# Text rows normalised by ScalarE, VectorE's token-stage order following TensorE's products, and another bank order in attention's first product

## The chip, the cores and the metric

The kernel runs on one core of a Trainium2 chip. The metric is the device time of one execution in microseconds (us). The core has five engines, each with its own queue of instructions that it takes strictly in order: TensorE (PE in the profile; its weight loads are PEld), VectorE (DVE), ScalarE (ACT), GpSimd (POOL) and SyncE (SP), which here only issues transfers. They are ordered against each other by semaphores alone: an instruction raises one when it ends, and another engine's queue stands at a wait until it is high enough.

## The reference

One transformer layer over 16 sequences of 69 tokens of width 256, in fp32. A sequence is one class token, 36 image patches and 32 text rows.

```
h = tokens(x)                      # per patch: 768 values
    x = layernorm(x; ln1_g, ln1_b) @ W + bias
    x = layernorm(x; ln2_g, ln2_b) + pe
h = concat(cls, h, txt)            # 16 x 69 x 256
h = h + attention(layernorm(h))    # one head, rotated q and k, softmax
h = h + ffn(layernorm(h))          # shared expert + best 2 of 8 experts
```

The layernorm in front of attention has no gain and no shift: `(h - mean) / sqrt(var + eps)`. For the text rows it depends on the input alone, so it can be done while the patches are still being worked on.

## The kernel before

The whole layer is one program. Its stages are tokens (0 to some 44 us), attention (to some 85 us), the shared expert with the router (to some 160 us), and the routed experts, 25 tiles of 128 rows (to the end). Every stage is a list of calls per engine, written out by hand; the order of the calls in each engine's list is the order of its queue. Between engines there are only the semaphores.

**Token stage.** The 576 patch rows lie in five tiles i = 0 to 4, the first of 64 rows and four of 128. For each tile:

- VectorE: `tok_stats(i)`, mean and variance of 768 values (L1175); GpSimd: `tok_root(i)`, the power -1/2 (L501, by L474); VectorE: `tok_shift(i)`, -mean times root (L1184); ScalarE: `tok_norm(i)`, scale and bias in place (L650).
- TensorE: `tok_transposes(i)`, six transposes (L859, by L853) into banks 2 and 3 for even i, 6 and 7 for odd i; ScalarE: `tok_turned(i)` takes them out with gain and shift of the first layernorm (L656); it counts `t_aff`.
- TensorE: `tok_product(i)`, bias and six products (L876, L881) into bank 4 for even i and 5 for odd i; it counts `t_mm`.
- VectorE: `tok_stats2(i)` (L1190): statistics of the product, then L1199, which takes it out of the bank with the second gain and counts `t_gain`. GpSimd: `tok_root2(i)`. VectorE: `tok_end(i)` (L1209), times the root, plus `pe`, into which GpSimd's `place_rows_of(i)` (L492) has added the second shift; it counts `t_done`.
- VectorE: `attention_front(i)` (L1214), statistics of the finished token rows; GpSimd: `attention_root(i)`; VectorE: `attention_bias(i)` (L1224); ScalarE: `attention_norm(i)` (L670).
- TensorE: `attention_transposes(k)` (L884): k = 0 to 3 are the four tiles of text rows, k = 4 to 8 the five token tiles, into bank 0 or 1. ScalarE: `attention_copy(k)` (L676) writes the high part (rounded to fp32r), VectorE: `attention_low(k)` (L1240) the rest, and counts `a_low`. Transposes k wait for `a_low` k - 1, since they write the bank of k - 2.

**Text rows.** `xtxt` holds 512 text rows as four tiles of 128 x 256. VectorE does `text_stats` (L1227) behind `tok_shift(2)`. GpSimd's `text_norm` (L481) takes one root for all four, waits for it, and normalises the tiles one after another (L486); each counts `x_normed`. It stands between `tok_root(2)` and `tok_root(3)`.

**Attention's weights.** wq, wk and wv are split in the same way, GpSimd making the high part (L496, L498), VectorE the low part (L1246, L1247, in one call `attention_weights`, counting `a_w` once).

**Attention's first product.** The 16 sequences are four groups of four (276 columns). `attention_qk(g)` (L898) has two halves `eo`, each of two products (q and k) of six matmuls; half 1 writes banks 4 and 5, half 0 banks 2 and 3, and half 1 comes first. Group 0 waits ahead of everything for `a_low` 6, `a_w` 1, `t_aff` 5 and `t_gain` 5. VectorE's rotation, `attention_turn(0)` (L1257, L1258) and `attention_rope(0)` (L1261, L1262), waits for all four products; `attention_v(0)` and `attention_scores(0)` follow on TensorE.

**Order around the change.** GpSimd's list begins at L526. After `attention_root(4)` it waits for `a_w`, `t_mm` 5 and `t_done` 5, and then splits the first experts' weights in pieces of 128 x 512 (L442, L443) between the roots of attention's second layernorm (`flat_root(g)`). `load_weights(n)` (L432) issues the transfer of 1 MB of expert weights into one of two stages. ScalarE's list begins at L725, TensorE's at L1037, VectorE's at L1314. SP issues all input transfers in a fixed order and then, tile by tile behind `t_done`, the copies of the token rows into `h` (`place_images`, L351).

## Time and profile before

| | |
|---|---|
| median of 3 runs | 341.75 us (339.48 to 342.25) |
| the profiled execution: its own time | 340.2 us |
| its span in the profile | 338.4 us |
| TensorE busy | 301.1 us (89%) |
| VectorE, ScalarE, GpSimd busy | 159.8, 145.3, 210.0 us |

The profiled execution is one more run beside the three. Its span goes from the first instruction to the last, and all times within the profile count from the span's start; around the span lie 1.8 us of the execution's own time. In a timeline, consecutive instructions of one line are merged into a row with their count; the start is that of the first, the time is from there to the end of the last. "Idle before" is how long the engine had stood, and the arrow names what ended that. The duration of a matmul record overlaps with the next one's. PEclk is TensorE's granted clock as a share of 2.4 GHz.

### The profile page before, as it was taken

The numbers are of one execution on the slowest core, as the hardware profiler recorded it, in microseconds if no ns is written. First come the engines' busy times: TensorE is split into PE (matmuls) and PEld (weight loads), VectorE is DVE, ScalarE is ACT, GpSimd is POOL, SyncE is SP. The second block draws the span as 40 slices with busy tenths as digits, with TensorE's granted clock in tenths as the row PEclk, the third lists the DMA queues.
The fourth block names the chain that finished last, engine by engine and source line by source line (L and its number), as shares of the span: only waits on it lengthen the run. The fifth ranks groups of instructions, "written<-read, shape, count | busy, mean of one in ns | idle before, by whom it ended". The sixth has DMA issues, their size and how long they took to land.

```text
span 338.4 us, 6655 instructions
## 1 busy us (share of the span) xinstructions
PE 301.1 (89%) x2049; PEld 269.5 (80%) x2050; DVE 159.8 (47%) x402; ACT 145.3 (43%) x327; POOL 210.0 (62%) x168
## 2 busy tenths in 40 slices
PE   0879788998897969999899999999999999999970
PEld 0456587887795969998699989998999899899960
DVE  3558867888853399473223332433233233323220
ACT  2647313375978533642444344333433343344210
POOL 2476373148882000755988988898888899335551
PEclk9997979999999999999999999999999999999997
DMA  7955404002464230375453364255333633224522
GB/s 235 314 104 158 144 26 158 0 27 63 153 211 157 97 119 2 108 239 193 164 169 108 137 201 163 52 172 186 114 111 101 175 57 47 34 44 47 64 33 31
DMA packets 21926, 39.91 MB, mean 118 GB/s; under 512 B 2914, under 2 KB 18227, under 8 KB 19603
## 3 DMA queue, kind: packets, MB, share of 16 engines
q0 software_dynamic: 7456, 25.43, 28.0%
q1 hardware_dynamic: 14162, 14.03, 13.4%
q10 hardware_dynamic: 288, 0.20, 0.2%
q8 instruction: 11, 0.18, 0.2%
q14 instruction: 9, 0.07, 0.1%
HBM read 28.84 MB, written 6.93 MB: 106 GB/s over the span
## 4 chain that ended last, share of the span: by engine, by line
PE 41%; POOL 12%; DMA 12%; issue 8%; DVE 7%; ACT 2%; POOLq 2%; SPq 0%; DVEq 0%; ACTq 0%
DMA out_tokens<-xy_all,dest 11%; PE ps L978 9%; PE ps L979 9%; PE ps L980 9%; PE ps L1028 7%; POOL ring L443 6%; PE ps L853 4%; POOL ring L442 3%; POOL out_tokens L590 2%; PE ps L948 2%; POOLq L587 1%; PE ps L1100 1%; DVE h L1286 1%; DVE ps L1258 1%; DVE qk L1257 1%
## 5 line engine op out<-in xcount | busy, mean ns | idle before, releaser
L443 POOL TENSOR_TENSOR ring<-stage,ring 128x512 fp32r<-128x512 f32 (+2 forms) x30 | 76.2, 2541 | 2.5
L1549 DVE TENSOR_TENSOR hgT<-ps,hgT 128x512 fp32r<-128x512 f32 x50 | 32.2, 687 | 72.2 <-ACT hgT L843 72.2
L978 PE MATMUL ps<-ring,hgT 128*128 x200 | 58.0, 290 | 2.1 <-DVE xy_all L1555 1.5
L590 POOL DMA_INDIRECT out_tokens<-xy_all,dest x25 | 39.5, 1582 | 27.5 <-DMA out_tokens<-xy_all,dest 15.6
L980 PE MATMUL ps<-ring,hgT 128*128 x200 | 55.9, 279 | 0.0
L979 PE MATMUL ps<-ring,hgT 128*128 x200 | 55.9, 279 | 0.0
L835 ACT ACTIVATE hg<-ps 128x512 f32<-128x512 f32 x50 | 29.9, 599 | 47.6 <-PE ps L980 47.6
L580 POOL DMA_INDIRECT xy_all<-normalized_tokens,dest x25 | 24.9, 997 | 38.8 <-DVE dest L1511 31.4
L978 PE MATMUL ps<-ring,xgT 128*128 x100 | 41.3, 413 | 1.1 <-issue 0.6
L442 POOL TENSOR_SCALAR ring<-stage 128x512 fp32r<-128x512 f32 (+2 forms) x30 | 38.5, 1284 | 2.6 <-PEq L1114 2.4
L978 PEld LDWEIGHTS ps<-ring,hgT 128*128 128x128 f32 x200 | 37.6, 188 | 2.6 <-issue 2.6
L979 PE MATMUL ps<-ring,xgT 128*128 x100 | 39.4, 394 | 0.0
L980 PE MATMUL ps<-ring,xgT 128*128 x100 | 39.2, 392 | 0.0
L979 PEld LDWEIGHTS ps<-ring,hgT 128*128 128x128 f32 x200 | 37.7, 188 | 0.0
L980 PEld LDWEIGHTS ps<-ring,hgT 128*128 128x128 f32 x200 | 37.6, 188 | 0.0
L818 ACT ACTIVATE xgT<-ps 128x256 fp32r<-128x256 f32 x25 | 9.6, 386 | 53.7 <-PE ps L853 53.7
L1555 DVE TENSOR_SCALAR xy_all<-ps,gate 128x256 f32 (+1 forms) x25 | 12.1, 484 | 38.6 <-PE ps L980 38.6
L1028 PE MATMUL ps<-ring,hid 128*128 128x256 f32 x216 | 29.5, 282 | 0.2 <-DVE base L1378 0.2
L1028 PEld LDWEIGHTS ps<-ring,hid 128*128 128x128 f32 x216 | 28.3, 189 | 0.6 <-issue 0.5
L843 ACT ACTIVATE hgT<-ps 128x512 fp32r<-128x512 f32 x50 | 27.1, 599 | 2.6 <-PE ps L853 2.6
L853 PE MATMUL ps<-mats,hg 128*128 128x128 f32 x200 | 25.9, 272 | 0.0
L853 PEld LDWEIGHTS ps<-mats,hg 128*128 128x128 f32 x200 | 23.3, 140 | 3.2
(193 smaller groups left out, 591.0 us busy)
## 6 DMA issues: line engine op xcount, KB each, us to landing
stage<-in_w_up POOLq DMA_DIRECT2D x9, 1024.0 KB, 5.5
stage<-in_w_dn POOLq DMA_DIRECT2D x9, 1024.0 KB, 5.6
xg<-xy_all SPq DMA_DIRECT2D x25, 128.0 KB, 2.7
xp<-in_patches SPq DMA_DIRECT2D x4, 384.0 KB, 7.6
normalized_tokens<-hn SPq DMA_DIRECT2D x4, 276.0 KB
residual_tokens<-h SPq DMA_DIRECT2D x4, 276.0 KB
ring<-in_tok_w SPq DMA_DIRECT2D x1, 768.0 KB, 7.0
base<-residual_tokens SPq DMA_DIRECT2D x2, 384.0 KB, 4.1
```

Source lines behind the costliest of these rows:

```text
L442: link(nc.gpsimd.tensor_scalar(hi, stage[:, part, c0:c1], 1.0, 0.0, ALU.mult, ALU.add))
L443: return nc.gpsimd.tensor_tensor(lo, stage[:, part, c0:c1], hi.bitcast(F32), ALU.subtract)
L580: pool.indirect_dma_start(xy_all[:, t, :], None, xn_d, bass.IndirectOffsetOnAxis(ap=dest[:, t:t + 1].bitcast(U32), axis=0)).then_inc(rows_ ...
L590: pool.indirect_dma_start(out, bass.IndirectOffsetOnAxis(ap=dest[:, t:t + 1].bitcast(U32), axis=0), xy_all[:, t, :], None, compute_op=ALU. ...
L835: nc.scalar.activation(hg[:, 1 - c, 512 * half:512 * (half + 1)], ps[:, hidden_bank + half, :], ACT.Gelu).then_inc(e_act, 1)
L843: nc.scalar.activation(hgT[:, c, 0, 4 * half:4 * half + 4, :], ps[:, turned_bank + half, :].rearrange("p (k t) -> p k t", k=4), ACT.Copy). ...
L853: return nc.tensor.transpose(o, i, ident[0:n, 0:n])
L978: nc.tensor.matmul(o, a[0], b[0], start=n == 0, stop=False)
L979: nc.tensor.matmul(o, a[0], b[1], start=False, stop=False)
L980: last = nc.tensor.matmul(o, a[1], b[0], start=False, stop=n == len(pairs) - 1)
L1028: last = nc.tensor.matmul(ps[:, down_bank[j], 0:D], a[x], b[y], start=f == 0 and m == 0, stop=f == KF - 1 and m == 2)
L1549: v.tensor_tensor(hgT[:, c, 1, 4 * half:4 * half + 4, :], ps[:, turned_bank + half, :].rearrange("p (k t) -> p k t", k=4), hgT[:, c, 0, 4 ...
```

## The change

It does three things. Of the text rows GpSimd keeps the root alone; VectorE works out -mean times root for all four tiles in one operation (`text_shift`, into the new `xnb`), and ScalarE normalises two tiles behind `tok_norm(2)` and two behind `attention_copy(1)`. The low part of attention's weights is made in three calls (half of the q and k weights by `w` each, then v), each counting `a_w`, and VectorE's and GpSimd's lists are put in another order; on GpSimd `load_weights(0)`, `load_weights(1)`, `attention_weights` and `place_rows_of(i)` move. ScalarE takes `attention_copy(2)` ahead of `tok_turned(3)`. In `attention_qk(0)` the half on banks 2 and 3 comes first, the wait for `t_gain` stands ahead of the second half, and the wait for the v weights stands ahead of `attention_v(0)`. TensorE's list is the same.

```diff
--- before.py
+++ after.py
@@ -160,6 +160,7 @@
         xst = sb("xst", [P, NG, 6], where=slots12)
         xmv = sb("xmv", [P, NG, 2], where=slots12)
         xrs = sb("xrs", [P, NG], where=slots12)
+        xnb = sb("xnb", [P, NG], where=slots12)
         pr = sb("pr", [SEQ, GB, SEQ], where=slots12)
         asm = sb("asm", [SEQ, 3, GB], where=slots12)
         prT = sb("prT", [SEQ, GB, SEQ], where=slots12)
@@ -213,7 +214,7 @@
         first_in = sem("first_in")
         pe_in, rope_in, text_in = [sem(f"pe_in{i}") for i in range(NPT)], sem("rope_in"), sem("text_in")
         rows_of_text_in = sem("rows_of_text_in")
-        x_stats, x_rstd, x_normed = sem("text_stats"), sem("text_rstd"), sem("text_normed")
+        x_stats, x_rstd, x_shift, x_normed = (sem(n) for n in ("text_stats", "text_rstd", "text_shift", "text_normed"))
         img_in = [sem(f"img_in{i}") for i in range(NPT)]
         a_stats, a_rstd, a_normed, a_tr, a_hT = (sem(n) for n in ("a_stats", "a_rstd", "a_normed", "a_tr", "a_hT"))
         a_norm_in, a_low, a_whi, a_w = sem("a_norm_in"), sem("a_low"), sem("a_whi"), sem("a_w")
@@ -478,13 +479,9 @@
                 r = AROWS[i]
                 root(ars[0:r, i:i + 1], amv[0:r, i, 1:2], r, a_rstd)
 
-            def text_norm():
+            def text_root():
                 pool.wait_ge(x_stats, 1)
                 root(xrs[:, :], xmv[:, :, 1], P, x_rstd)
-                pool.wait_ge(x_rstd, 1)
-                for j in range(NG):
-                    nc.gpsimd.tensor_scalar(xtxt[:, j, :], xtxt[:, j, :], xmv[:, j, 0:1], xrs[:, j:j + 1], ALU.subtract,
-                                            ALU.mult).then_inc(x_normed, 1)
 
             def place_rows_of(i):
                 pool.wait_ge(pe_in[i], 16 * (1 if i == 0 else 2))
@@ -527,29 +524,29 @@
             tok_root(0)
             tok_root(1)
             tok_root(2)
-            text_norm()
+            text_root()
             tok_root(3)
             pool.wait_ge(tok_vec_in, 32)
             place_rows_of(0)
             tok_root2(0)
+            load_weights(0)
             tok_root(4)
-            load_weights(0)
+            place_rows_of(1)
             attention_root(0)
-            place_rows_of(1)
+            attention_weights()
             tok_root2(1)
+            place_rows_of(2)
+            load_weights(1)
             attention_root(1)
-            attention_weights()
-            place_rows_of(2)
+            place_rows_of(3)
             tok_root2(2)
-            load_weights(1)
+            place_rows_of(4)
             attention_root(2)
-            place_rows_of(3)
             tok_root2(3)
             attention_root(3)
-            place_rows_of(4)
             tok_root2(4)
             attention_root(4)
-            pool.wait_ge(a_w, 1)
+            pool.wait_ge(a_w, 3)
             pool.wait_ge(t_mm, NPT)
             pool.wait_ge(t_done, NPT)
             piece(0, 0)
@@ -670,6 +667,12 @@
                 nc.scalar.activation(tn[0:r, i, :], tt[0:r, i, :], ACT.Identity, bias=anb[0:r, i:i + 1],
                                      scale=ars[0:r, i:i + 1]).then_inc(a_normed, 1)
 
+            def text_norm(j0, j1):
+                act.wait_ge(x_shift, 1)
+                for j in range(j0, j1):
+                    nc.scalar.activation(xtxt[:, j, :], xtxt[:, j, :], ACT.Identity, bias=xnb[:, j:j + 1],
+                                         scale=xrs[:, j:j + 1]).then_inc(x_normed, 1)
+
             def attention_copy(k):
                 act.wait_ge(a_tr, k + 1)
                 for o, i in placings(k, 0):
@@ -728,14 +731,16 @@
             tok_turned(0)
             tok_turned(1)
             tok_norm(2)
+            text_norm(0, 2)
             tok_norm(3)
             tok_turned(2)
             attention_copy(0)
             attention_copy(1)
+            text_norm(2, 4)
             tok_norm(4)
             attention_norm(0)
+            attention_copy(2)
             tok_turned(3)
-            attention_copy(2)
             attention_copy(3)
             attention_copy(4)
             attention_norm(1)
@@ -898,12 +903,13 @@
             def attention_qk(g):
                 te.wait_ge(a_low, NG + LAST_TILE[g] + 1)
                 if g == 0:
-                    te.wait_ge(a_w, 1)
+                    te.wait_ge(a_w, 2)
                     te.wait_ge(t_aff, NPT)
-                    te.wait_ge(t_gain, NPT)
                 else:
                     te.wait_ge(a_rope, g)
-                for eo in (1, 0):
+                for eo in (1, 0) if g else (0, 1):
+                    if g == 0 and eo == 1:
+                        te.wait_ge(t_gain, NPT)
                     if g >= 3 and eo == 0:
                         te.wait_ge(f_lo, g - 2)
                     for w in range(2):
@@ -914,6 +920,8 @@
 
             def attention_v(g):
 
+                if g == 0:
+                    te.wait_ge(a_w, 3)
                 if g >= 1:
                     te.wait_ge(a_exp, g)
                     te.wait_ge(a_pTs, g)
@@ -1234,18 +1242,24 @@
                 link(last)
                 v.tensor_scalar(xmv[:, :, 1], xmv[:, :, 1], EPS, None, ALU.add).then_inc(x_stats, 1)
 
+            def text_shift():
+                dve.wait_ge(x_rstd, 1)
+                v.scalar_tensor_tensor(out=xnb[:, :], in0=xmv[:, :, 0], scalar=-1.0, in1=xrs[:, :], op0=ALU.mult,
+                                       op1=ALU.mult).then_inc(x_shift, 1)
+
             def attention_low(k):
                 dve.wait_ge(a_hT, k + 1)
                 for (o, i), (high, _) in zip(placings(k, 1), placings(k, 0)):
                     last = v.tensor_tensor(o, i, high.bitcast(F32), ALU.subtract)
                 last.then_inc(a_low, 1)
 
-            def attention_weights():
-
+            def attention_weights(n):
                 dve.wait_ge(a_whi, 1)
-                v.tensor_tensor(wqk2[:, 1, :, :, :], wqk[:, :, :, :], wqk2[:, 0, :, :, :].bitcast(F32), ALU.subtract)
-                v.tensor_tensor(wv2[:, 1, :, :], wvs[:, :, :], wv2[:, 0, :, :].bitcast(F32),
-                                ALU.subtract).then_inc(a_w, 1)
+                if n < 2:
+                    v.tensor_tensor(wqk2[:, 1, n, :, :], wqk[:, n, :, :], wqk2[:, 0, n, :, :].bitcast(F32),
+                                    ALU.subtract).then_inc(a_w, 1)
+                else:
+                    v.tensor_tensor(wv2[:, 1, :, :], wvs[:, :, :], wv2[:, 0, :, :].bitcast(F32), ALU.subtract).then_inc(a_w, 1)
 
             def attention_turn(g):
                 if g == 0:
@@ -1319,6 +1333,7 @@
             tok_shift(2)
             text_stats()
             tok_stats(3)
+            text_shift()
             tok_shift(3)
             tok_stats2(0)
             tok_stats(4)
@@ -1329,26 +1344,28 @@
             attention_low(1)
             attention_bias(0)
             tok_stats2(1)
+            attention_weights(0)
             tok_end(1)
             attention_front(1)
+            attention_weights(1)
+            attention_bias(1)
             attention_low(2)
+            tok_stats2(2)
             attention_low(3)
-            attention_bias(1)
-            tok_stats2(2)
-            attention_weights()
-            attention_low(4)
             tok_end(2)
             attention_front(2)
+            attention_low(4)
             attention_bias(2)
+            attention_weights(2)
             tok_stats2(3)
             attention_low(5)
             tok_end(3)
             attention_front(3)
+            tok_stats2(4)
             attention_bias(3)
-            tok_stats2(4)
-            attention_low(6)
             tok_end(4)
             attention_front(4)
+            attention_low(6)
             attention_bias(4)
             attention_turn(0)
             attention_rope(0)
```

## Rows read from the trace of the kernel before

**Rows 1.** Windows: us, busy of each engine, PEclk, DMA share, GB/s
```profile
45.00:46.00 1.00, 1.00 (x6) 1.00 (x6) 0.52 (x1) 0.00 (x0) 1.00 (x2) 0.50 0.08 21
200.00:320.00 120.00, 120.00 (x829) 109.90 (x829) 39.13 (x71) 45.73 (x89) 93.50 (x52) 1.00 0.42 98
...
```

**Rows 2.** Timeline, TensorE: start, us, what, count, [idle before, releaser]
```profile
12.87 4.91 PE L881 MATMUL ps<-ring,xT 128*64 128x256 f32 x12
...
25.91 0.74 PE L853 MATMUL ps<-mats,xtxt 128*128 128x128 f32 x4 [2.43 <-DVE hT_n L1240]
...
27.21 4.54 PE L881 MATMUL ps<-ring,xT 128*128 128x256 f32 x12
31.59 0.29 PE L853 MATMUL ps<-mats,tn 65*128 65x65 f32 x2
...
33.09 2.86 PE L881 MATMUL ps<-ring,xT 128*128 128x256 f32 x12
...
39.41 0.38 PE L853 MATMUL ps<-mats,tn 128*128 128x128 f32 x2
43.25 0.36 PE L978 MATMUL ps<-hT_n,wqk 128*128 128x276 f32 x1 [3.46 <-DVE tt L1199]
...
53.32 0.38 PE L978 MATMUL ps<-hT_n,wqk 128*128 128x276 f32 x1
...
56.45 0.41 PE L853 MATMUL ps<-mats,pr 69*69 69x69 f32 x4
...
```

**Rows 3.** Timeline, GpSimd, 0 to 72 us
```profile
14.29 1.01 POOL L474 TENSOR_TENSOR xrs<-xmv,half_neg 128x4 f32<-128x4 f32 x1 [2.21 <-DVE xmv L1235]
15.41 4.85 POOL L486 TENSOR_SCALAR xtxt<-xtxt,xmv,xrs 128x256 f32<-128x256 f32 x4
20.23 0.55 POOL L474 TENSOR_TENSOR trs<-tmv,half_neg 128x1 f32<-128x1 f32 x1
20.76 0.71 POOL L492 TENSOR_TENSOR ring<-ring,vecs 64x256 f32<-64x256 f32 x1
...
30.11 1.04 POOL L496 TENSOR_SCALAR wqk<-ring 128x1024 fp32r<-128x1024 f32 x1
...
45.43 0.62 POOL L442 TENSOR_SCALAR ring<-stage 128x512 fp32r<-128x512 f32 x1
...
66.45 1.04 POOL L474 TENSOR_TENSOR rs<-mv,half_neg 69x4 f32<-69x4 f32 x1 [12.27 <-DVE mv L1299]
...
```

**Rows 4.** Timeline, VectorE, 0 to 66 us
```profile
20.81 0.68 DVE L1187 SCALAR_TENSOR_TENSOR tnb<-tmv,trs 128x1 f32<-128x1 f32 x1 [4.64 <-POOL trs L474]
...
22.54 1.00 DVE L1179 BATCH_NORM_STATS2 tst<-xp 128x6 f32<-128x384 f32 x2
...
24.00 0.51 DVE L1209 SCALAR_TENSOR_TENSOR tt<-tt,trs,ring 65x256 f32<-65x256 f32 x1
...
25.21 0.15 DVE L1219 TENSOR_SCALAR amv<-amv 65x1 f32<-65x1 f32 x1
...
32.93 1.22 DVE L1246 TENSOR_TENSOR wqk<-ring,wqk 128x1024 fp32r<-128x1024 f32 x1
...
37.69 0.42 DVE L1196 BATCH_NORM_STATS2 tst<-ps 128x6 f32<-128x256 f32 x1
...
38.82 0.55 DVE L1240 TENSOR_TENSOR hT_n<-ps,hT_n 128x16 fp32r<-128x16 f32 x3
...
48.18 1.31 DVE L1257 TENSOR_TENSOR qk<-ps,rope 128x1104 f32<-128x1104 f32 x1 [2.13 <-PE ps L980]
...
```

**Rows 5.** Timeline, ScalarE, 0 to 66 us
```profile
21.53 1.03 ACT L653 ACTIVATE xp<-xp,tnb,trs 128x768 f32<-128x768 f32 x1 [6.45 <-DVE tnb L1187]
...
42.00 0.60 ACT L670 ACTIVATE tn<-tt,anb,ars 128x256 f32<-128x256 f32 x1 [1.66 <-DVE anb L1224]
...
```

**Rows 6.** Timeline of SP; DMA issues: count, KB, us to landing
```profile
9.37 0.55 SPq L345 DMA_DIRECT2D ring<-in_wv  x1
...
ring<-in_wv SPq DMA_DIRECT2D x1, 256.0 KB, 9.7
...
```

## The prediction

> **What bounds the kernel now.** I read the windows first, then the timelines of the first 66 us engine by engine. From 200 to 320 us TensorE is busy 120.00 of 120.00 us at clock 1.00 [rows 1]: the experts run at TensorE's pace, so nothing in this change shortens them, and they start when the work ahead hands over. The change lies in the first 48 us, where TensorE is not full. Its timeline shows two holes [rows 2]: 2.43 us before the text transposes at 25.91, released by VectorE's low part of the turned rows, and 3.46 us before attention's first product at 43.25, released by VectorE's L1199, the gain of the last token tile. Behind each hole the work runs slowly: the 12 matmul records of the third token product take 4.54 us where the fourth's take 2.86 [rows 2], and in 45 to 46 us the granted clock is 0.50 [rows 1], that is 1.2 GHz where 2.4 was granted before the hole. So in this stretch VectorE sets the time, and the text rows sit at its head: GpSimd takes 4.85 us for four text rows from 15.41, only then the root of tile 3 at 20.23 [rows 3], and VectorE waits 4.64 us for it (from 16.17 to 20.81) [rows 4] and ScalarE 6.45 us (from 15.08 to 21.53) [rows 5].
>
> **The text rows.** GpSimd loses 4.85 us. ScalarE gains four operations of 128x256 with scale and bias; the same form in attention_norm takes 0.60 [rows 5], starts 0.5 apart when they queue, so 2.2 us in two pairs. This form on xtxt isn't in the trace; the bounds are 0 (wholly inside ScalarE's 6.45 us idle) and 4.85 (GpSimd's pace); I take 0, since its first pair needs xrs (14.29 + 1.01 = 15.3) [rows 3] and xnb. xnb is one new VectorE operation of four columns behind tok_stats(3), at 16.2, some 0.15. The new operation can cost 0.15 (shift(3) is held for another reason at that time) or, held by GpSimd like the row discussed next, 0.7; neither moves tok_norm(3) by more than 0.5. ScalarE then: text pair 16.35 to 17.4, tok_norm(3) 17.6 to 18.6, tok_turned(2) and two copies to 21.4, second text pair to 22.4, tok_norm(4) to 23.4. Nothing behind them is late: TensorE needs tile 3 at 22.5, behind its second product, as now.
>
> **VectorE's new order, forward from 16.2.** Root(3) runs 16.25 to 16.8 (0.55 [rows 3]), not from 20.23. Tok_shift(3) is held to 17.5, and here a row counts that is easily missed: tnb at 20.81 took 0.68 us for one column, while GpSimd's L492 ran from 20.76 for 0.71; both ended together [rows 3, 4]. A VectorE operation with two inputs in SBUF stands until GpSimd's running operation has ended. I charge this hold wherever it falls; its bounds are 0 and 1.04, GpSimd's longest operation here [rows 3].
> The Trainium skill, page "SBUF — State Buffer", section "Who interferes with whom", says that the two engines share one pair of ports and that whichever starts first holds it for its whole instruction, so that GpSimd can be the one that waits. The row above agrees for GpSimd first; no row here shows VectorE first. By the rule place_rows_of(2) would be pushed behind attention_weights(0), and my sum would change by 0.3 us at most.
> Steps (start on VectorE; lengths by rows 4): tok_stats2(0) at 17.8, when the first product ends (12.87 + 4.91 [rows 2]), 1.13 (37.69 to 38.82); tok_stats(4) 1.46 (22.54 to 24.00), to 20.4; tok_end(0) and attention_front(0) 1.36 (24.00 to 25.36), to 21.8; shift(4), low(0), low(1) 0.9, to 22.7. Attention_root(0) ends 22.4, but GpSimd then copies wqk for 1.04 [rows 3]: bias(0) ends 23.45. Tok_stats2(1) to 24.6. Attention_weights(0) is half of the 1.22 row [rows 4]: to 25.2. Tok_end(1) is held by place_rows_of(2) (24.9 to 25.6), and with front(1) ends 27.0; weights(1) to 27.6; bias(1) behind root(1) and place_rows_of(3) 28.3; low(2) to 28.7 (ScalarE's copy(2), now ahead of tok_turned(3), is done at 24.4; behind it, as before, it would be 26.5, still in time). There TensorE's attention_transposes(4) can start, now at 31.59 [rows 2]: **2.9 us earlier**.
> Is TensorE ready? Its second text pair comes at 23.2, not 25.91; the third product, 5.68 us from 25.91 to 31.59 with 1.68 lost to the clock (4.54 less 2.86), is through at 27.2. It waits 1.5 us for low(2).
> From transposes(4) on TensorE's queue is full: 31.59 to 39.41 is 7.8 us [rows 2], so transposes(6) come at 36.5. Their inputs are ready (low(3) 30.2 for 32.9; low(4) 32.4 for 36.5).
>
> **Attention's first product.** Today it waits for t_gain of tile 4. Banks 2 and 3 don't hold that product, so with them first only low(5) (35.1), a_w 2 (27.6) and the last turned tile (32) are needed: it starts at 36.85 instead of 43.25. The gap of 3.84 us behind transposes(6) (39.41 to 43.25) shrinks to 0.35: **3.5 us**. The other two banks come 1.56 us later, 38.4; t_gain is there at 36.5 + 1.13 = 37.65. The product itself takes 3.13 at full clock, as qk(1) does (53.32 to 56.45) [rows 2], and ends at 40.0. Against now (43.25 to the rotation at 48.18 [rows 4], 4.9) that is 1.8 less; but bias(4) stands ahead of the rotation in VectorE's queue: tok_end(4) waits for its root (38.0), front(4) ends 39.4, root(4) 39.95, and the weights' first piece, 0.62 [rows 3], holds bias(4) to 40.6. So **1.2 us**. The rotation starts at 40.6 instead of 48.18: 2.9 + 3.5 + 1.2 = **7.6 us**.
>
> **What else moves.** Splitting the weights' low part into three adds two fixed parts of 0.1 us, inside the above. A_w 3 falls at 33.4, ahead of its waiters: the values at 40.4 and GpSimd's pieces at 39.95. GpSimd's first weight load goes from behind root(4) to behind tok_root2(0), about 19.3. The last wide input, wv, is issued at 9.37 and lands 9.7 later, 19.1 [rows 6]; its reader is at 23.4. SP's queue keeps its order and its waits (t_done) fall earlier. Behind 48 us nothing is edited. GpSimd waits 12.27 us for VectorE at 66.45 [rows 3], so its pieces have room, and with experts at TensorE's pace the whole 7.6 should arrive at the end. I charge nothing for it; the bounds are 0 and 7.6 lost.
> The profiled execution took 340.2 us (span 338.4); less 7.6 it gives 332.6. The median shown is 341.75, 1.55 more; less 7.6 it gives 334.15. I forecast between them, **333.4 us**.
>
> **The rivals.** A: a low clock remains. TensorE's hole of 1.5 us is shorter than the two behind which it fell (2.43, 3.46), but they are of one order, and the level was low after both. One fall costs what it cost now, 1.7 us; two 3.4: 335 to 337. Chance 0.16.
> B: the holds don't fall as charged (bias(0) 0.75, tok_end(1) 0.4, bias(1) 0.7, bias(4) 0.6). Then TensorE's third product binds, at 27.2: 1.5 for it and 0.6 for the last: 331.3. Chance 0.14.
> C: the earlier start isn't handed on: a wait on a DMA or on GpSimd's splitting takes its place between 50 and 160 us. Against it: the 12.27 us of room, and no loads bound there. Up to all of 7.6 goes: 337 to 341. Chance 0.07.
> D, the slower side, by the clock alone: the hole before transposes(4) grows past 2.43 us, and the clock stays low to the end of the first value product. Products 3 and 4 cost 1.7 more each, qk(0) at most its own 3.1 again, the values 2.9 (24 matmuls of 256 columns for 276), the hole 1.2: 10.6 of loss against 7.6, so 343 us, with the median's offset 344. It decides once the loss passes 7.6. Against it: the fall at the third product cost 1.68, half of 3.4 us at half rate, and the fourth product ran at full rate again. Chance 0.03. The forecast keeps 0.60.
>
> **Range and chances.** Low end B less a little, 330.5; high end A with two falls and part of C, 338.5. A measurement of this kernel tells about 1%, 3.4 us: faster by more means below 338.3, which holds the forecast, A and B but for strays and a part of C: 0.87. Within 1%: 0.09. Slower: 0.04.
>
> **What would show it.** In the changed kernel's timelines: tnb of tile 3 near 17.5; xtxt on ScalarE at 16.4 and 21.4, 0.60 each; transposes(4) near 28.7 released by VectorE's hT_n; the first qk matmul near 36.9 with almost no idle before it, on banks 2 and 3; granted clock 1.00 from 24 to 45; the rotation at 40.6; the values' and the experts' rows all 7 to 8 us earlier. Wrong would be: ScalarE busy with text rows when tok_norm(3) could run, transposes(4) later than 30, the product at 37 standing for t_gain, or equal first rotations and unequal ends, which is C.

## The result, and the profile after

The changed kernel takes 338.06 us (337.42 to 339.28, 10 runs), the kernel before 341.12 us (339.48 to 343.18, 10 runs) beside it: a ratio of 0.9916 with the interval 0.9892 to 0.9941. It gains 3.06 us where 7.6 were forecast. The direction was right, the size was not. The time lies inside the stated range of 330.5 to 338.5 us, near its slow end, and by the ratio the gain is 0.84%, an outcome ("within 1%") that had been given 0.09. The profiled execution of the changed kernel took 339.28 us, with a span of 337.4; the one before took 340.2, so these two differ by 0.9 us only. Throughout, executions more than 1.5% above the fastest of their kernel belong to a second, slower state and are left out of medians and ratios.

Where the 7.6 us were to come from, VectorE's timeline of the changed kernel, in the order of time (lines: L1247 the new `text_shift`, L1195 the shift of a token tile, L1232 `attention_bias`, L1259 the low part of the q and k weights, L1217 `tok_end`, L1253 `attention_low`, L1271 the rotation):

```profile
16.34 0.15 DVE L1247 SCALAR_TENSOR_TENSOR xnb<-xmv,xrs 128x4 f32<-128x4 f32 x1
17.09 0.68 DVE L1195 SCALAR_TENSOR_TENSOR tnb<-tmv,trs 128x1 f32<-128x1 f32 x1 [0.59 <-POOL trs L475]
...
22.49 1.53 DVE L1232 SCALAR_TENSOR_TENSOR anb<-amv,ars 65x1 f32<-65x1 f32 x1
...
25.07 0.68 DVE L1259 TENSOR_TENSOR wqk<-ring,wqk 128x512 fp32r<-128x512 f32 x1
25.67 0.95 DVE L1217 SCALAR_TENSOR_TENSOR tt<-tt,trs,ring 128x256 f32<-128x256 f32 x1
...
27.40 0.68 DVE L1259 TENSOR_TENSOR wqk<-ring,wqk 128x512 fp32r<-128x512 f32 x1
28.55 0.68 DVE L1232 SCALAR_TENSOR_TENSOR anb<-amv,ars 128x1 f32<-128x1 f32 x1 [0.46 <-POOL ars L475]
29.15 0.41 DVE L1253 TENSOR_TENSOR hT_n<-ps,hT_n 128x256 fp32r<-128x256 f32 x1
...
44.56 0.57 DVE L1232 SCALAR_TENSOR_TENSOR anb<-amv,ars 128x1 f32<-128x1 f32 x1 [0.20 <-POOL ars L475]
45.05 1.29 DVE L1271 TENSOR_TENSOR qk<-ps,rope 128x1104 f32<-128x1104 f32 x1
```

The rotation begins at 45.05 and not at 48.18 [rows 4]: 3.13 us earlier, near the gain of the medians. That the two agree is in part chance: the profiled execution lost 2.2 of the 3.13 us again later, which is taken up below. The head of the list went as forecast: VectorE had stood 4.64 us ahead of tile 3's shift [rows 4], and now the shift is done at 17.77. The text rows are on ScalarE, in its timeline:

```profile
16.53 1.09 ACT L673 ACTIVATE xtxt<-xtxt,xnb,xrs 128x256 f32<-128x256 f32 x2 [1.59 <-DVE xnb L1247]
17.80 1.03 ACT L650 ACTIVATE xp<-xp,tnb,trs 128x768 f32<-128x768 f32 x1 [0.17 <-DVE tnb L1195]
...
21.32 1.13 ACT L673 ACTIVATE xtxt<-xtxt,xnb,xrs 128x256 f32<-128x256 f32 x2
```

Two pairs of 1.1 us, at the places and of the length forecast, and the wide normalisation at 17.80 waits for VectorE's shift and not for the text pair: the text rows cost nothing there. Then TensorE's timeline, which answers to [rows 2]:

```profile
23.67 2.86 PE L886 MATMUL ps<-ring,xT 128*128 128x256 f32 x12
29.71 0.31 PE L858 MATMUL ps<-mats,tn 65*128 65x65 f32 x2 [3.18 <-DVE hT_n L1253]
29.85 1.27 PE L858 MATMUL ps<-mats,xp 128*128 128x128 f32 x6
31.05 1.22 PE L881 MATMUL ps<-biasr,mats 1*128 1x256 f32 x2
32.20 5.18 PE L886 MATMUL ps<-ring,xT 128*128 128x256 f32 x12
...
40.85 0.38 PE L858 MATMUL ps<-mats,tn 128*128 128x128 f32 x2
40.99 0.37 PE L986 MATMUL ps<-hT_n,wqk 128*128 128x276 f32 x1
```

The third token product now runs at 23.67 in 2.86 us, at full rate, where it took 4.54 at 27.21 [rows 2]. But behind it TensorE stands 3.18 us, more than the 2.43 of the hole before the change, released by `attention_low(2)`; and the next product takes 5.18 us for the same 12 records. The windows say why (columns as in [rows 1]):

```profile
30.00:31.00 1.00, 1.00 (x7) 0.72 (x5) 0.96 (x5) 0.91 (x4) 0.62 (x2) 0.55 0.91 373
31.00:36.00 5.00, 5.00 (x12) 3.58 (x12) 2.81 (x10) 2.80 (x7) 1.17 (x2) 0.50 0.18 50
36.00:37.00 1.00, 1.00 (x3) 0.79 (x3) 0.00 (x0) 0.00 (x0) 0.00 (x0) 0.53 0.00 0
```

The granted clock is 0.50 to 0.55 from 30 to 37 us, that is 1.2 GHz. The low stretch costs 3.4 us (the seven windows lack 0.45 + 5 x 0.50 + 0.47): from `attention_transposes(4)` to `attention_transposes(6)` are 11.14 us where they were 7.82 [rows 2]. The change took away two holes, of 2.43 and 3.46 us, and put one of 3.18 in their place. The last two rows of the timeline show the bank order at work: the attention product starts 0.14 us behind transposes(6), where 3.84 us lay between them.

### The profile page after: what moved, and what is told of

It reads as the page before. It is cut to its first block, busy times and chain, and to the rows that moved or that the text cites. A ratio compares the mean times of both kernels' runs of the same rounds, so it can differ in the third digit from the quotient of the medians.

```text
span 337.4 us, 6656 instructions
## 1 busy us (share of the span) xinstructions
PE 302.1 (90%) x2049; PEld 270.4 (80%) x2050; DVE 162.0 (48%) x404; ACT 147.7 (44%) x331; POOL 206.2 (61%) x164
## 4 chain that ended last, share of the span: by engine, by line
PE 43%; POOL 13%; DMA 11%; issue 10%; DVE 9%; ACT 3%; POOLq 3%; SPq 0%; DVEq 0%; ACTq 0%
DMA out_tokens<-xy_all,dest 10%; PE ps L986 9%; PE ps L987 8%; PE ps L988 8%; PE ps L1036 7%; POOL ring L444 6%; PE ps L858 4%; POOL ring L443 3%; POOL out_tokens L587 3%; PE ps L886 2%; POOLq L584 2%; PE ps L956 2%; PE ps L1108 1%; DVE h L1300 1%; DVE ps L1272 1%
## 5 line engine op out<-in xcount | busy, mean ns | idle before, releaser
L587 POOL DMA_INDIRECT out_tokens<-xy_all,dest x25 | 39.5, 1582 | 27.6 <-DMA out_tokens<-xy_all,dest 15.3
L1036 PE MATMUL ps<-ring,hid 128*128 128x256 f32 x216 | 30.2, 287 | 0.2 <-DVE base L1395 0.2
L1036 PEld LDWEIGHTS ps<-ring,hid 128*128 128x128 f32 x216 | 29.2, 194 | 0.6 <-issue 0.5
```

Source lines behind the costliest of these rows:

```text
L587: pool.indirect_dma_start(out, bass.IndirectOffsetOnAxis(ap=dest[:, t:t + 1].bitcast(U32), axis=0), xy_all[:, t, :], None, compute_op=ALU. ...
L1036: last = nc.tensor.matmul(ps[:, down_bank[j], 0:D], a[x], b[y], start=f == 0 and m == 0, stop=f == KF - 1 and m == 2)
```

## The experiments

Four questions. Is it the hole and its clock that ate the gain? Is it the new order that makes the hole? What is each of the three parts worth alone? Is there a version better than both? Ratios are to the kernel before, run beside each batch (its medians 341.25 us beside e1 to e4, 341.10 beside e5 to e8, 340.43 beside e9 to e11), with their 95% intervals. Experiments of different batches are compared by their ratios. One part in a hundred of the ratio is 3.4 us.

### Is it the hole?

**e3_hole_filled**: the changed kernel, and TensorE does six unread fp32 products in the hole. They are extra work, in a bank part that nothing reads.

```diff
             tok_product(2)
+            te.wait_ge(t_gain, 2)
+            for n in range(6):
+                nc.tensor.matmul(ps[:, 5, 256:512], ones, mats[:, 1:3, :]..., start=True, stop=True)
             attention_transposes(4)
```

> The changed kernel with six matmuls whose result nobody reads (128x256, 0.48 us each, some 2.9 us) in TensorE's hole ahead of transposes(4). Nothing else starts earlier by that. Theory clock: transposes(4) stay at 29.7, but the third-to-last stretch runs at clock 1.00 (the product 2.86 instead of 5.18, the transposes and bias 1.0 less), attention's product starts near 37.7 and the rotation near 41.8: 3.3 us faster than the changed kernel, 334.8. Rival, VectorE or a transfer bounds the stretch and TensorE's long records only stretch over it: same as the changed kernel, 338.

Measured: 335.39 us (335.02 to 336.07), ratio 0.9814 [0.9775, 0.9853]. TensorE's timeline of e3:

```profile
26.23 2.75 PE L1059 MATMUL ps<-mats 128*128 128x256 f32 x12
29.30 0.31 PE L858 MATMUL ps<-mats,tn 65*128 65x65 f32 x2 [0.32 <-DVE hT_n L1256]
...
30.83 2.86 PE L886 MATMUL ps<-ring,xT 128*128 128x256 f32 x12
...
37.16 0.38 PE L858 MATMUL ps<-mats,tn 128*128 128x128 f32 x2
```

The filler rows (twelve records for six products) are 2.75 us of work added, and the kernel is faster than the changed one, by 3.5 us as the ratios give it and 2.7 as the medians do. Transposes(4) start where they did (29.30 for 29.71), but the product behind them takes 2.86 for 5.18, and transposes(6) come 7.86 us later and not 11.14. So the clock behind the hole, and not the hole's own length, took most of what was missing.

**e4_low2_early**: the changed kernel, one call moved on VectorE.

```diff
             tok_stats2(1)
+            attention_low(2)
             attention_weights(0)
             tok_end(1)
             attention_front(1)
             attention_weights(1)
             attention_bias(1)
-            attention_low(2)
```

> The changed kernel with VectorE's attention_low(2) ahead of attention_weights(0) instead of behind attention_bias(1). Theory: transposes(4) start at 26.6 behind the third product with no hole, the clock stays at 1.00, and VectorE is what is late next (tok_end and front of tile 4, bias(4)): rotation at 41 to 41.5, 334 to 334.5 us. Rival, the order only trades one VectorE wait for another (transposes(5) stand for low(3), the hole moves there): 337 to 338.

Measured: 334.77 us (334.22 to 335.27), ratio 0.9792 [0.9753, 0.9830]. TensorE's timeline of e4, and the row of its rotation from VectorE's:

```profile
23.30 2.86 PE L886 MATMUL ps<-ring,xT 128*128 128x256 f32 x12
25.99 0.28 PE L858 MATMUL ps<-mats,tn 65*128 65x65 f32 x2
```

```profile
40.42 1.29 DVE L1271 TENSOR_TENSOR qk<-ps,rope 128x1104 f32<-128x1104 f32 x1
```

With `attention_low(2)` ahead of the weights there is no hole ahead of transposes(4): they follow the product, and in its profile no window is below 1.00 up to the last matmul. The rotation begins at 40.42; the forecast's place for it was 40.6. The hole was made by the order of five calls on VectorE, none of which TensorE needed so soon.

**e9_copies_early** keeps the order on VectorE and takes the longest hold out of it: GpSimd copies the weights ahead of `tok_root(4)`.

```diff
             load_weights(0)
+            attention_weights()
             tok_root(4)
             place_rows_of(1)
             attention_root(0)
-            attention_weights()
```

> The changed kernel with GpSimd's two copies of the attention weights ahead of tok_root(4) and nothing else. Theory, the holds made the hole: bias(0) takes 0.15 instead of 1.53, low(2) and transposes(4) come at 28.2 instead of 29.7, the hole is 1.7 us instead of 3.2. If the clock outlasts that: rotation at 41, 334.8 us. If it falls behind 1.7 us too: 1.4 us from the hole alone, 336.7, or with a short fall 335 to 337. Rival, bias(0) was not on the path: 338, as the changed kernel.

Measured: 336.66 us (333.23 to 337.76), ratio 0.9869 [0.9827, 0.9911]. TensorE's timeline of e9:

```profile
29.31 0.31 PE L858 MATMUL ps<-mats,tn 65*128 65x65 f32 x2 [1.78 <-DVE hT_n L1253]
...
30.84 4.54 PE L886 MATMUL ps<-ring,xT 128*128 128x256 f32 x12
```

The hold of bias(0) is gone (0.14 us, at 23.49), but transposes(4) come no earlier for it: 29.31, where e3, which keeps the hold, has 29.30. The move delays tile 4's shift by the copies, and what VectorE gained by the one it lost by the other. The hole is down to 1.78 us because the third product is 1.0 us later (24.67), and not because the transposes are ready sooner, as was expected. It is near the 1.5 of the forecast, and still the clock fell behind it, for the smaller price: 4.54 and not 5.18, with a granted clock of 0.50 from 31 to 34. This profiled run had a second fall, at 102 to 107; five of the six runs show a mean granted clock of 0.983 or 0.984 and take 336.4 to 337.8 us, the sixth shows 0.993 and takes 333.23. One kernel, two times 3.4 us apart, by whether the clock fell. (Each run's result gives its mean granted clock; over a span of 335 us, 0.005 of it is one price of 1.7 us. The profiled executions without a fall up to the last matmul show 0.991 to 0.993, since the clock also falls behind it, where that costs nothing.)

### Does the same hold for the kernel before?

**e8_before_filled**: the kernel before, with four unread products ahead of `attention_transposes(2)` and six ahead of attention's first product.

```diff
             tok_transposes(3)
+            te.wait_ge(t_gain, 1)
+            for n in range(4): ...
             attention_transposes(2)
...
             attention_transposes(6)
+            te.wait_ge(t_aff, NPT)
+            for n in range(6): ...
             attention_qk(0)
```

> The kernel before with matmuls whose result nobody reads in its two holes: four (some 1.9 us) ahead of transposes(2), six (2.9 us) ahead of attention's first product. Theory clock: both falls go (1.7 us each, by the sum of what the granted clock lacks), nothing else changes: rotation at 44.9 instead of 48.18, 337.7. Rival, the falls in before lay beside VectorE's work and cost less than they measure: 339 to 341.

Measured: 339.45 us (339.23 to 340.40), ratio 0.9958 [0.9939, 0.9976]: 1.4 us by the ratio where 3.4 were expected. TensorE's timeline of e8:

```profile
25.98 0.74 PE L853 MATMUL ps<-mats,xtxt 128*128 128x128 f32 x4 [0.70 <-DVE hT_n L1246]
...
27.28 2.86 PE L881 MATMUL ps<-ring,xT 128*128 128x256 f32 x12
30.39 0.31 PE L853 MATMUL ps<-mats,tn 65*128 65x65 f32 x2 [0.26 <-DVE hT_n L1246]
...
42.70 0.36 PE L978 MATMUL ps<-hT_n,wqk 128*128 128x276 f32 x1 [1.49 <-DVE tt L1205]
```

No window of it is below 1.00 up to the last matmul, so both falls are gone. Transposes(4) start 1.2 us earlier than at 31.59 [rows 2], but the attention product only 0.55 earlier than at 43.25: between them it is VectorE that sets the time, and it had not been waiting for the slow product long. The second fall was on the path in full: the rotation stands 2.08 us earlier (46.10 for 48.18 [rows 4]), 0.55 of it from the start of the product and 1.5 from its rate. The price of a low clock is 1.7 us of TensorE's time, but what it costs the kernel is what of it lies ahead of the engine that is waited for.

### What each part is worth

**e1_banks_only**: the kernel before with the bank order alone.

```diff
-                    te.wait_ge(t_gain, NPT)
...
-                for eo in (1, 0):
+                for eo in (1, 0) if g else (0, 1):
+                    if g == 0 and eo == 1:
+                        te.wait_ge(t_gain, NPT)
```

> The kernel before with nothing but the bank order of attention's first product. If the banks carry the gain on their own: the product starts at 39.8 instead of 43.25, the hole and with it the low clock go, its second half waits for t_gain at 43.05, and the rotation waits for bias(4) at 46.05 instead of 48.18: 2.1 us faster than before, 339.0. If VectorE's order has to come first, since bias(4) is late either way: under 0.5 us.

Measured: 341.33 us (339.55 to 344.20), ratio 0.9998 [0.9958, 1.0039]: nothing. TensorE's timeline of e1:

```profile
26.02 0.99 PE L853 MATMUL ps<-mats,xtxt 128*128 128x128 f32 x4 [2.42 <-DVE hT_n L1241]
...
28.09 5.33 PE L881 MATMUL ps<-ring,xT 128*128 128x256 f32 x12
33.25 0.29 PE L853 MATMUL ps<-mats,tn 65*128 65x65 f32 x2
...
44.83 0.40 PE L979 MATMUL ps<-hT_n,wqk 128*128 128x276 f32 x1 [1.84 <-DVE tt L1200]
```

The first half does start behind transposes(6), and the hole of 3.46 us shrinks to 1.84 before the second half, with no fall behind it. But the first hole, the same as before to 0.01 us (2.42 for 2.43), is here followed by twice the low stretch: 5.33 us for the product and not 4.54, and transposes(4) 1.66 later than before. So the rotation gains only 0.54 (47.64). What the banks gave, the other fall took, in this profiled run; the 12 runs spread over 4.7 us.

**e2_banks_undone**: the changed kernel with the old bank order and its wait.

```diff
+                    te.wait_ge(t_gain, NPT)
...
-                for eo in (1, 0) if g else (0, 1):
-                    if g == 0 and eo == 1:
-                        te.wait_ge(t_gain, NPT)
+                for eo in (1, 0):
```

> The changed kernel with the old bank order. The product waits for t_gain at 42.2 instead of starting at 41.0; with the clock up it ends 45.4, and the rotation begins at 45.5 instead of 45.05: 0.4 us slower than the changed kernel, 338.5. If that hole of 1.2 us is enough to bring the clock down again: 2 us slower, 340.

Measured: 339.87 us (339.20 to 342.33), ratio 0.9964 [0.9932, 0.9997]; by the ratios 1.6 us more than the whole change, with intervals that just overlap. In its TensorE timeline the first attention product waits again:

```profile
30.03 0.31 PE L858 MATMUL ps<-mats,tn 65*128 65x65 f32 x2 [2.73 <-DVE hT_n L1252]
...
31.56 4.54 PE L886 MATMUL ps<-ring,xT 128*128 128x256 f32 x12
...
41.14 0.37 PE L985 MATMUL ps<-hT_n,wqk 128*128 128x276 f32 x1 [1.19 <-DVE tt L1206]
```

Here the low stretch behind the hole of 2.73 us is the short one, which gives back 1.7 of what the wait costs in this trace (rotation at 44.53), while the medians go against it; this run has a second fall at 103 to 107. The clearer measure of the banks is e10 against e6 below, which differ by them alone: 0.9816 against 0.9891, 2.6 us.

**e6_text_only**: the kernel before with the text rows on ScalarE and nothing else (the text parts of the change's diff; every other call stays where it was).

```diff
-            text_norm()
+            text_root()
...
             tok_norm(2)
+            text_norm(0, 2)
...
             attention_copy(1)
+            text_norm(2, 4)
...
             tok_stats(3)
+            text_shift()
```

> The kernel before with nothing but the text rows on ScalarE (text_shift on VectorE behind tok_stats(3)). VectorE's old order has low(2) ahead of bias(1) and the weights' low part, so by forward steps transposes(4) come at 26.6 with no hole; the hole moves to attention's first product, which waits for t_gain from 35.1 to 39.5; one fall there, rotation at 44.4 instead of 48.18: 337.3. Rival, the text rows are of use only with VectorE's new order: within 1 us of before, 341.

Measured: 337.35 us (336.62 to 338.00), ratio 0.9891 [0.9862, 0.9919]. One third of the change gives as much as the whole (0.9916 [0.9892, 0.9941]), and by the middle of the intervals 0.8 us more. TensorE's timeline of e6:

```profile
26.31 0.31 PE L858 MATMUL ps<-mats,tn 65*128 65x65 f32 x2 [0.40 <-DVE hT_n L1250]
...
38.42 0.36 PE L983 MATMUL ps<-hT_n,wqk 128*128 128x276 f32 x1 [3.87 <-DVE tt L1204]
```

With the old order of VectorE's list transposes(4) come at 26.31, 3.4 us before those of the changed kernel, and the first hole is 0.40. What is left is the hole of 3.87 before attention's product and the clock behind it (below 1.00 from 39 to 43): just what the other bank order is for.

**e5_text_back**: e4 with the text rows back on GpSimd.

```diff
-            text_root()
+            text_norm()
...
-            text_norm(0, 2)
...
-            text_norm(2, 4)
...
-            text_shift()
```

> Experiment e4 with the text rows given back to GpSimd (text_norm there, no text_shift), all orders kept. Theory: root(3) at 20.2 again, transposes(2) at 25.8 behind a hole of 2.4 us, one fall of the clock there; rotation at 44 instead of 40.4, 336.5 to 338.5 us. Rival, once VectorE's order is right the text rows don't matter: within 1 us of e4, under 335.8.

Measured: 339.04 us (337.94 to 341.14), ratio 0.9937 [0.9909, 0.9964]: by the ratios 4.9 us above e4. Its rotation begins at 44.02, 3.6 later than e4's. The text rows are worth 3.7 us in the one surrounding (e6) and 4.9 in the other. One row of it went against its expectation, that a fall follows the hole ahead of transposes(2), TensorE's timeline of e5:

```profile
25.33 0.74 PE L860 MATMUL ps<-mats,xtxt 128*128 128x128 f32 x4 [2.07 <-DVE hT_n L1255]
...
26.63 2.86 PE L888 MATMUL ps<-ring,xT 128*128 128x256 f32 x12
```

The product behind the hole of 2.07 us runs at full rate. The one fall of this profile lies at 48 to 52, behind the rotation.

### A better version

**e10_text_and_banks**: e6 with e1's bank order; VectorE's and GpSimd's lists are those of before, but for the text rows. It puts together two parts that gave 3.7 us and nothing.

```diff
-                for eo in (1, 0):
+                for eo in (1, 0) if g else (0, 1):
+                    if g == 0 and eo == 1:
+                        te.wait_ge(t_gain, NPT)
```

> Experiment e6 with the bank order: both edits of the change but none of its reordering. By forward steps no hole ahead of transposes(4), attention's first product at 34.6 instead of 38.4, its second half behind t_gain at 38.2, rotation at 41.2 instead of 43.35, no fall: 335.2. If the 2 us wait between the product's halves brings the clock down: 336.9.

**e11_and_bias4_behind**: e10 with `attention_bias(4)` between the two halves of the rotation, where GpSimd's first piece of weights can't hold the rotation up.

```diff
-            attention_bias(4)
             attention_turn(0)
+            attention_bias(4)
             attention_rope(0)
```

> Experiment e10 with VectorE's bias(4) behind the first half of the rotation. Rotation at 39.9 instead of 41.2; TensorE waits for transposes(8) instead, still ahead of the scores: 1.0 to 1.3 us faster than e10, 334.1. Rival, transposes(8) or the values come late for it: as e10.

Measured: e10 334.50 us (333.79 to 335.59, five runs), ratio 0.9816 [0.9789, 0.9843]; e11 334.35 us (333.89 to 334.50, five runs), ratio 0.9814 [0.9788, 0.9841]. Both beat both kernels: 5.9 and 6.1 us less than the 340.43 beside them, twice the gain of the change, and as good as e4 with its whole reordering. The held bias of 0.57 us is out of the way in e11's trace (rotation at 40.59 and not 41.20), but the 1.0 to 1.3 us expected of it didn't come: the medians differ by 0.15. The two are one kernel up to 40 us, and their TensorE rows give the plainest view of the clock. e10's timeline, the first and the last record of the second half:

```profile
38.38 0.39 PE L984 MATMUL ps<-hT_n,wqk 128*128 128x276 f32 x1 [1.94 <-DVE tt L1205]
...
40.07 0.43 PE L986 MATMUL ps<-hT_n,wqk 128*128 128x276 f32 x1
```

and e11's:

```profile
38.68 0.40 PE L984 MATMUL ps<-hT_n,wqk 128*128 128x276 f32 x1 [1.92 <-DVE tt L1205]
...
40.20 0.29 PE L986 MATMUL ps<-hT_n,wqk 128*128 128x276 f32 x1
```

Holes of 1.94 and 1.92 us in the same place; 1.3 us behind the one the clock fell (39.26 to 39.51 still run at full rate), behind the other it didn't. e10's profile has a second fall, at 101 to 105.

**e7_two_more_moves**: e4 with both small moves, e9's and e11's.

```diff
             load_weights(0)
+            attention_weights()
             tok_root(4)
...
             attention_turn(0)
+            attention_bias(4)
             attention_rope(0)
```

> Experiment e4 with two more moves against GpSimd's holds: its copies of the attention weights ahead of tok_root(4), so that bias(0) isn't held for 1.5 us, and VectorE's bias(4) behind the first half of the rotation, which then starts when the product ends. Rotation at 39.0 to 39.4 instead of 40.4: 333.6 us. Rival, the held operations were not on the path: 334.8 as e4.

Measured: 335.44 us (333.86 to 337.87), ratio 0.9845 [0.9805, 0.9885]. Its profile has the earliest rotation of all, 39.00, and with 331.8 us the shortest span of all the profiles; but its six runs lie over 4 us, and by the median nothing is gained over e4. The mean clock of the runs orders them: three at 0.991 to 0.993 take 333.86 to 334.77, two at 0.987 take 336.12 and 336.41, one at 0.978 takes 337.87. So the moves earn some 0.4 us where no clock is lost, and in half of the runs it is lost; where in the kernel, only a profile of such a run would show, and there is none.

## Why the prediction was wrong in size

**The text rows.** Right: four operations of 0.59 to 0.64 us inside ScalarE's idle time, tile 3's shift at 17.77 for a forecast 17.5 (the 0.68 us hold included), the third product 0.7 us from where the steps put it. Alone they give 3.7 us (e6).

**Attention's first product.** Right: it starts behind transposes(6) with nothing between, on the other banks, and the second half is not held. The 3.5 us were there. Of the 1.2 us 0.9 came: from the product's start to the rotation are 4.06 us where they were 4.93, with the hold of bias(4) (0.57, from 44.56) and the product at full rate.

**VectorE's new order: the step that failed.** "There TensorE's attention_transposes(4) can start, now at 31.59 [rows 2]: 2.9 us earlier", and "It waits 1.5 us for low(2)", with nothing in the sum for the clock behind that wait. It started 1.9 us earlier, at 29.71, waited 3.18, and the clock behind it cost 3.4. Two terms were off, and both have one root: the prediction stepped through the new list alone. Through the old list, with the text rows on ScalarE, transposes(4) come at 26.31 (e6), so the term for the order should have been a loss and not a gain.

First, the holds. VectorE's bias(0) was charged up to the end of the wqk copy, 23.45. GpSimd's timeline:

```profile
22.38 1.04 POOL L493 TENSOR_SCALAR wqk<-ring 128x1024 fp32r<-128x1024 f32 x1
23.40 0.61 POOL L495 TENSOR_SCALAR wv<-ring 128x512 fp32r<-128x512 f32 x1
...
25.36 0.97 POOL L489 TENSOR_TENSOR ring<-ring,vecs 128x256 f32<-128x256 f32 x1
...
27.58 0.94 POOL L475 TENSOR_TENSOR ars<-amv,half_neg 128x1 f32<-128x1 f32 x1 [0.67 <-DVE amv L1227]
```

The bias stood from 22.49 to 24.02, through both copies, since the second began as the first ended: 0.57 more than charged, and 1.38 of hold beyond its own 0.15, more than the stated bound of 1.04. Weights(0) end at 25.75 for 25.2, and that 0.55 stays up to the second weights (28.08 for 27.6). Then the hold works in the other direction. GpSimd's root at 27.58 met VectorE's second weights (27.40 to 28.08) and took 0.94 for 0.55; bias(1) waited for it, started at 28.55 and stood behind the next row placement (28.49 to 29.20): it ends 0.93 late, at 29.23 for 28.3. The placement at 25.36 shows the same, 0.97 where it takes 0.71 alone [rows 3], from meeting the first weights. VectorE first and GpSimd waiting is the Trainium skill's rule (page "SBUF — State Buffer", section "Who interferes with whom": issue order decides who blocks). The prediction had no row for it; here are these two, 0.39 and 0.26 us, and with what queues behind it the late part grew by 0.4, where the prediction allowed 0.3 at most. This chain is read from one trace: e9, which took bias(0)'s hold away, lost as much elsewhere, so no run shows by itself what that hold was worth. The hole is then 1.5 of the forecast, 1.0 of late start, and 0.7 because the third product ended at 26.5 and not 27.2: an engine that is ready sooner has a longer hole.

Second, and larger, the clock. The forecast had it at 1.00 from 24 to 45 us because the hole was to be 1.5 us. Rival A said "one fall costs what it cost now, 1.7 us" and gave it 0.16. The fall came, and cost 3.4: transposes(6) at 40.85 instead of 36.5 is 1.0 of late start and 3.3 of clock. The rotation at 45.05 instead of 40.6 is then 1.0 + 3.3 and 0.15 of small change. e3 gives back the clock alone, and it confirms the rest of the sum: from transposes(4) to the rotation it takes 12.06 us (29.30 to 41.36) where the forecast had 11.9 (28.7 to 40.6). e4 gives back the clock and the late start, but that its 40.42 falls on the 40.6 is luck: its transposes(4) start at 25.99, 2.7 us ahead of the forecast's, and VectorE, which is then the one that is waited for, takes those 2.7 us back. So rival A's mechanism decided, at twice its price. The hole had also grown, as rival D named it, but a hole of 2.42 us has cost one price and two, so that its length doubled the price is not shown. The cause is what e4 moved: the five calls ahead of low(2). Why the fall cost two prices and not one stays open.

**Handed on to the end.** Not in full: the prediction charged nothing here, and rival C doubted it. Of e4's 7.76 us at the rotation 5.98 arrive in the profiled times (334.22 for 340.2). Its lead is 7.2 us in the shared expert at 113.09 (for 120.29) and 6.03 at one addition of VectorE's there, ahead of which VectorE stands 2.33 us in e4 and 1.11 before. VectorE's timeline, before and then e4:

```profile
143.67 1.08 DVE L1378 TENSOR_TENSOR base<-base,ps 128x256 f32<-128x256 f32 x3 [1.11 <-PE ps L1028]
```

```profile
137.64 1.08 DVE L1395 TENSOR_TENSOR base<-base,ps 128x256 f32<-128x256 f32 x3 [2.33 <-PE ps L1036]
```

Why it is 1.2 us later there was not found; e3 shows the same 2.31 us, and in e11 VectorE stands 1.12 there. e11 has lost 1.4 of its 7.59 us by 114 us (114.11 for 120.29) and loses nothing at this place.

**The order as a whole.** e10 has the old order and stands at 0.9816; e4 has the new one mended and stands at 0.9792; the intervals overlap. The new order, in the form of the change, costs some 3.4 us against e10 (by the ratios), and mended it gives nothing that these runs can tell.

## What to carry to other kernels

When a change moves an engine's list, ask of every call that is put ahead whether TensorE waits next for one behind it, and step through the old list as well as the new one. Price a hole of TensorE at its length and the possible fall behind it, and try a version that fills or closes it before the parts are weighed against each other, since a fall in one place can hide what a part gives in another (e1). Take a bundle apart: here one part gave as much as the three together, and two of them twice as much.

## What the runs showed of the hardware that was not expected

**The price of a fall has two sizes and does not follow the hole's length.** The same hole of 2.42 to 2.43 us was followed by a product of 4.54 us [rows 2] and of 5.33 (e1). Holes of 1.78 (e9) and 1.94 (e10) had a fall behind them, holes of 1.92 (e11) and 2.07 (e5) none. Summed over the 1-us windows of a profile up to its last matmul, the missing clock is 0 (e3, e4, e7, e8, e11), 1.7 (e5, e6), 3.4 (before, e1, e2, e9, e10) or 5.1 us (the changed kernel): always a whole number of 1.7, within 0.02. What decides it at a given hole the runs don't tell. Behind the last matmul the clock falls in every profile, 2.2 us (e3) to 4.9 us (the changed kernel) after it.

**It also falls with no hole that long.** The last 1.7 of the changed kernel's 5.1 us lie at 132 to 136, in the shared expert, as 36 narrow products of 50 columns (128.35 to 132.57) end; the last idle time of TensorE ahead of them was 0.77 us, at 123.62. The kernel before has the same products and the same 0.77 and no fall there. The lead over it shrinks in this stretch from 2.52 us (117.77 for 120.29) to 1.00 (143.90 for 144.90). The four of the ten runs with a mean clock of 0.979 or 0.980, the profiled one among them, take 338.43 to 339.28 us, and of the other six five take 337.42 to 337.69. A window of it:

```profile
133.00:135.00 2.00, 2.00 (x9) 2.00 (x8) 0.16 (x2) 0.41 (x2) 1.25 (x2) 0.50 0.00 0
```

Three more falls, at 101 to 107 in e2, e9 and e10, began 2.3 to 2.6 us behind the start of the router's products, ahead of which TensorE had stood 1.48 to 1.54 us; before the change the same place has 1.50 us and no fall. In e5 it fell behind 1.82 us of idle ahead of 48.13, and in e4 1.80 us at the same place had none.

**Falls make the spread, and they differ from run to run.** e3 and e4, at 0.990 to 0.993 in every run, spread over 1.05 us each; e1's twelve runs go from 0.992 (339.83 us) to 0.971 (344.20 and 344.02) and spread over 4.7. One profile is one such run: e10's, at 0.984, is its slower kind, while four others of it, at 0.992 to 0.994, take 333.79 to 334.71. The changed kernel never got past 0.985 in ten runs. That agrees with a loss behind its hole in every run, though only the profiled one shows where the clock fell.

**A hold can last over several operations of the other engine.** One VectorE operation of a single column stood 1.53 us behind two GpSimd copies in a row; without a neighbour it takes 0.15. The other way round, GpSimd's root at 28.20 in e6 took 1.52 us where 0.55 is its own time, beside VectorE's low part of wqk (28.02 to 29.32).
